# Layer 1's expert rows: added to the output in memory block by block, where they were kept apart and combined at the end

## What is computed

```python
probs = jax.nn.softmax(scores)
weights, idx = jax.lax.top_k(probs, TOP_K)             # TOP_K = 2
weights = weights / jnp.sum(weights, axis=-1, keepdims=True)
out_all = jnp.einsum('tef,edf->ted', silu(xf @ w1) * (xf @ w3), w2)
expert_outs = jnp.take_along_axis(out_all, idx[:, :, None], axis=1)
result = jnp.einsum('tkd,tk->td', expert_outs, weights)
x = x + L1_attn(xn) + result
```

## Time and profile before

| | us |
|---|---|
| three executions: lowest, median, highest | 1772.83, 1775.10, 1778.98 |
| span of the profiled execution, first to last instruction | 1724.1 |
| PE busy in it | 1679.7 (97%) |
| DVE, ACT, POOL busy | 1350.6, 812.6, 609.5 |
| first and last put issued (start) | 1476.6 and 1679.9 |

### The profile page before, as it was taken

The page is one execution under the profiler, slowest core; times in us unless marked ns, Lnnn a source line. Parts: engine busy times, 40 slices in busy tenths (PEclk is TensorE's granted clock), DMA queues, the critical chain, the costliest instruction groups (busy, mean ns, idle before and its releaser), DMA issues.

```text
span 1724.1 us, 24432 instructions
## 1 busy us (share of the span) xinstructions
PE 1679.7 (97%) x7020; PEld 1188.6 (69%) x7020; DVE 1350.6 (78%) x3866; ACT 812.6 (47%) x1456; POOL 609.5 (35%) x656
## 2 busy tenths in 40 slices
PE   5999999999999999999999999999999999999995
PEld 4667777777777777777777777777777766667773
DVE  5878888888888787979797979787888776565558
ACT  4535453636363545454544445454545343554431
POOL 3311242424242324233333232332323233567770
PEclk8999999999999999999999999999999999999998
DMA  8949474646373747373737373645546445577758
GB/s 211 201 104 256 100 187 105 178 109 181 99 181 101 182 103 194 97 200 86 202 84 192 85 189 90 174 106 135 144 106 167 99 109 154 191 266 266 237 173 312
DMA packets 172339, 273.89 MB, mean 159 GB/s; under 512 B 14312, under 2 KB 57320, under 8 KB 171952
## 3 DMA queue, kind: packets, MB, share of 16 engines
q1 hardware_dynamic: 163632, 254.63, 56.1%
q0 software_dynamic: 8576, 17.70, 3.2%
HBM read 202.15 MB, written 65.93 MB: 155 GB/s over the span
## 4 chain that ended last, share of the span: by engine, by line
PE 94%; DVE 2%; ACT 1%; issue 1%; DMA 1%; POOL 0%; SPq 0%; POOLq 0%; DVEq 0%; ACTq 0%
PE ps_y L709 26%; PE ps_gate L660 8%; PE ps_gate L661 8%; PE ps_gate L662 8%; PE ps_up L662 8%; PE ps_up L660 8%; PE ps_up L661 8%; PE ps_y L735 4%; PE ps_side L675 3%; PE ps_side L758 1%; PE ps_side L852 1%; PE ps_side L835 1%; PE ps_side L794 1%; PE ps_side L819 1%; PE ps_side L660 1%; PE ps_side L661 1%
## 5 line engine op out<-in xcount | busy, mean ns | idle before, releaser
L918 DVE TENSOR_TENSOR silu_h<-ps_up,silu_h 128x512 f32<-128x512 f32 x618 | 424.0, 686 | 295.3 <-ACT silu_h L1325 243.3
L1325 ACT ACTIVATE silu_h<-ps_gate 128x512 f32<-128x512 f32 x618 | 367.6, 598 | 567.4 <-PE ps_gate L662 565.1
L709 PE MATMUL ps_y<-silu_h,w_dn 128*128 128x512 f32 x1056 | 542.7, 595 | 3.0 <-DVE silu_h L912 3.0
L912 DVE TENSOR_TENSOR silu_h<-coef_b,silu_h 128x512 f32<-128x512 f32 x528 | 386.8, 732 | 13.0 <-DMA coef_b<-coef_kept 9.2
L660 PE MATMUL ps_gate<-xnT,w_gu 128*128 128x512 f32 x528 | 342.7, 649 | 0.0
L709 PEld LDWEIGHTS ps_y<-silu_h,w_dn 128*128 128x128 f32 x1056 | 199.7, 189 | 53.7 <-issue 7.7
L660 PE MATMUL ps_up<-xnT,w_gu 128*128 128x512 f32 x528 | 207.9, 394 | 4.6 <-DVE silu_h L918 4.6
L661 PE MATMUL ps_gate<-xnT,w_gu 128*128 128x512 f32 x528 | 209.4, 397 | 0.0
L662 PE MATMUL ps_gate<-xnT,w_gu 128*128 128x512 f32 x528 | 208.9, 396 | 0.0
L662 PE MATMUL ps_up<-xnT,w_gu 128*128 128x512 f32 x528 | 208.0, 394 | 0.0
L661 PE MATMUL ps_up<-xnT,w_gu 128*128 128x512 f32 x528 | 206.8, 392 | 0.0
(11 more groups left out here) (267 smaller groups left out, 2454.8 us busy)
## 6 DMA issues: line engine op xcount, KB each, us to landing
coef_b<-coef_kept SPq DMA_DIRECT2D x254, 512.0 KB, 6.8
slots_x<-empty SPq DMA_DIRECT2D x15, 2080.0 KB, 12.7
w_block<-w_kept SPq DMA_DIRECT2D x45, 512.0 KB, 3.9
xs<-slots_x SPq DMA_DIRECT2D x37, 260.0 KB, 3.8
y_back<-y_kept SPq DMA_DIRECT2D x15, 512.0 KB, 7.0
w_down<-in_ffn_w SPq DMA_DIRECT2D x45, 128.0 KB, 3.7
w_raw<-in_ffn_w SPq DMA_DIRECT2D x33, 128.0 KB, 7.9
xres<-in_x SPq DMA_DIRECT2D x16, 256.0 KB, 3.1
```

The lines of the kernel that those rows point to most:

```text
L709: eng.matmul(ps_y[:, :], w_dn[:, j], silu_h[:, g % HBUFS], start=j == 0, stop=last).then_inc(pe_down)
L912: eng.tensor_tensor(silu_h[:, s], coef_b[:, q % COEF_RING, k], silu_h[:, s], ALU.mult).then_inc(dve_h)
L918: eng.tensor_tensor(silu_h[:, s], ps_up[g % 2][:, :], silu_h[:, s], ALU.mult).then_inc(dve_h1)
L1325: eng.activation(silu_h[:, s], ps_gate[g % 2][:, :], ACT.Silu).then_inc(act_silu)
```

## The change

The buffers y_kept and x1_kept are gone, and so are `load_x1`, `load_y`, `combine` and `store_out`. `keep_x1` stores x1 of a chunk straight into the rows of the output (same size and place in SP's list). The number that `send` stores with a row is the token's row, the same for both picks; that of an empty slot is a row of the last chunk, whose rows are stored after everything else. The put is an indirect DMA that adds to the output in memory. As two blocks may add to the same row, the first put of block c waits until the four puts of block c - 1 have landed; the first one of all waits for the 15 stores of x1. DVE computes no row numbers any more: POOL's CAST takes them from xs, and so `load_rows` must also wait for the CAST of the block that was in that place. At the end SP waits for all puts and for `last`, and stores the last chunk.

```diff
 def keep_x1(c):
     eng.wait_ge(*read("mixl", c))
-    eng.dma_start(x1_kept[c].rearrange("(r p) d -> p r d", p=P), xres[:, c % RING]).then_inc(x1_out, 16)
+    eng.dma_start(out_rows[c], xres[:, c % RING]).then_inc(x1_out, 16)
...
-            for c in range(YRING):
-                load_y(c)
-            for c in range(SPARSE):
-                store_out(c)
-                if c + YRING < SPARSE:
-                    load_y(c + YRING)
-                if c == SPARSE - 4:
-                    eng.wait_ge(dve_last, 1)
-                    eng.dma_start(last_rows, xres[:, (CHUNKS - 1) % RING]).then_inc(stored, 16)
-            eng.wait_ge(stored, 16 * CHUNKS)
+            eng.wait_ge(dve_last, 1)
+            eng.dma_start(out_rows[CHUNKS - 1], xres[:, (CHUNKS - 1) % RING]).then_inc(stored, 16)
+            eng.wait_ge(stored, 16)
...
 def load_rows(eng, t):
     if t >= XPLACES:
         eng.wait_ge(*read("ysT", t - XPLACES))
+        eng.wait_ge(pool_y_to, (t - XPLACES) // 2 + 1)
...
 elif what.startswith("put"):
     if r == 0 and c % 2 == 0:
-        eng.wait_ge(dve_y_row, c + n)
+        for t in range(c, c + n):
+            eng.wait_ge(xs_in[t % XPLACES], 16 * (t // XPLACES + 1))
-        eng.tensor_copy(y_to[:, these], y_row[:, these]).then_inc(pool_y_to)
+        eng.tensor_copy(y_to[:, these], xs[:, these, :, P + 1]).then_inc(pool_y_to)
         eng.wait_ge(pool_y_to, c // 2 + 1)
+    if r == 0 and c == 0:
+        eng.wait_ge(x1_out, 16 * SPARSE)
+    elif r == 0:
+        eng.wait_ge(landed[(c - 1) % XPLACES], 16 * ROWS * ((c - 1) // XPLACES + 1))
     if r == 0:
         eng.wait_ge(*read("ysT", c))
-    eng.indirect_dma_start(y_kept, bass.IndirectOffsetOnAxis(y_to[:, c % XPLACES, r:r + 1], 0), ys[:, c % BUFS1, r], None).then_inc(landed[c % XPLACES], 16)
+    eng.indirect_dma_start(out, bass.IndirectOffsetOnAxis(y_to[:, c % XPLACES, r:r + 1], 0), ys[:, c % BUFS1, r], None,
+                           compute_op=ALU.add).then_inc(landed[c % XPLACES], 16)
```

More of the change, by code:

```diff
@@ L58 @@
 ROW1 = P + 2
-COMBINE = UNITS1 - 3
-COMBINED = STEPS - TILES - COMBINE
 KEY0 = 1 << 17
@@ L307, in build_program @@
         ffn0.close()
[L308 to L313, removed]
+        xs = sb("xs", [XPLACES, ROWS, ROW1])
+        xsT = sb("xsT", [XBUFS, 2, CHUNK], FP32R)
         w_block = sb("w_block", [BUFS1, HALVES1, 2, 2, P], FP32R)
@@ L334, in build_program @@
         part_in, w_kept_out = sem("part_in"), sem("w_kept_out")
-        zero_out, x1_out, gates_out, gates_in, x1_in, stored = (sem(n) for n in ("zero_out", "x1_out", "gates_out", "gates_in", "x1_in", "stored"))
+        zero_out, x1_out, gates_out, gates_in, stored = (sem(n) for n in ("zero_out", "x1_out", "gates_out", "gates_in", "stored"))
         sent = [sem("sent0"), sem("sent1")]
@@ L367, in build_program @@
         dve_add, act_msg, pool_heard = (sem(n) for n in ("dve_add", "act_msg", "pool_heard"))
-        act_xshi, dve_y_row, pool_y_to, dve_out, dve_last = (sem(n) for n in ("act_xshi", "dve_y_row", "pool_y_to", "dve_out", "dve_last"))
+        act_xshi, pool_y_to, dve_last = (sem(n) for n in ("act_xshi", "pool_y_to", "dve_last"))
         dve_own = sem("dve_own")
@@ L1259, in step @@
                     eng.tensor_scalar(block_row[:, :], begins[:, :], float(CHUNK), None, ALU.mult).then_inc(dve_table)
-                elif what == "combine":
-                    combine(c)
                 elif what == "last":
@@ L1271, in step @@
                         read("xsT", key)[0])
-                    eng.wait_ge(xs_in[key % XPLACES], 16 * (key // XPLACES + 1))
-                    if key > 0:
-                        eng.wait_ge(dve_y_row, key)
-                    if key >= XPLACES:
-                        eng.wait_ge(pool_y_to, (key - XPLACES) // 2 + 1)
-                    to = xs[:, key % XPLACES, :, P + 1]
-                    keep(eng.tensor_scalar(y_past[:, :], to, float(TOP1 * TOKENS), float(key * CHUNK), ALU.is_ge, ALU.mult))
-                    wait_own()
-                    eng.tensor_tensor(y_row[:, key % XPLACES], to, y_past[:, :], ALU.add).then_inc(dve_y_row)
                 elif what == "ys":
@@ L1287, in step @@
                                       xs[:, key % XPLACES, :, P].unsqueeze(2).to_broadcast([P, ROWS, P]), ALU.mult).then_inc(read("ysT", key)[0])
-            def combine(c):
-                if c == 0:
-                    eng.wait_ge(x1_in, 16 * SPARSE)
-                eng.wait_ge(y_in[c % YRING], 16 * (c // YRING + 1))
-                keep(eng.tensor_tensor(x1_at(c), y_back[:, c % YRING, 0], x1_at(c), ALU.add))
-                wait_own()
-                eng.tensor_tensor(x1_at(c), y_back[:, c % YRING, 1], x1_at(c), ALU.add).then_inc(dve_out)
             eng.memset(minus_half[:, :], -0.5)
@@ L1313, in vector @@
                     step(what, key)
-            for c in range(COMBINED, SPARSE):
-                combine(c)
         def scalar(eng):
@@ L1578, in step @@
                         eng.tensor_copy(rows1[:, c % 2, :, P], gw[:, :, k])
-                        eng.tensor_scalar(rows1[:, c % 2, :, P + 1], row_of, float(k * TOKENS + c * CHUNK), None, ALU.add).then_inc(pool_mark)
+                        eng.tensor_scalar(rows1[:, c % 2, :, P + 1], row_of, float(c * CHUNK), None, ALU.add).then_inc(pool_mark)
                         eng.wait_ge(dve_slot, c + 1)
@@ L1598, in gpsimd @@
                     eng.wait_ge(pool_clear, 1)
-                    eng.tensor_scalar(empty[:, :, P + 1], row_of, float(TOP1 * TOKENS), None, ALU.add).then_inc(pool_clear)
+                    eng.tensor_scalar(empty[:, :, P + 1], row_of, float(SPARSE * CHUNK), None, ALU.add).then_inc(pool_clear)
             for g in range(STEPS):
```

38 lines of the change are left out of this document (4 added, 34 removed).

## The result

The changed kernel takes 1880.0 us (1876.32 to 1881.07, four runs), beside 1775.4 for the kernel before in the same session: ratio 1.0587 [1.0569, 1.0604], slower. The predicted time was 1879.0. That closeness is not what it seems. In a later session the same two kernels gave 1879.8 and 1726.1, ratio 1.0887 [1.0869, 1.0905]: 154 us, where the prediction worked out 104. Of 57 executions of the kernel before in the three later sessions 55 took 1724.8 to 1727.6 us, but one took 1935.5 at a granted clock of 0.84 and one 3504.2; for the four of the first session, 1772.8 to 1779.0, no span or clock is on record that would say what made them longer.

The account below looks back on a forecast made before the run. PE bounds the blocks, DVE and transfers the end; afterwards the chain of landings sets the pace. Span 1511.4 + 36 L = 1828.2 us with L = 8.8, plus 51.0 outside the span: 1879.2 us, range 1805 to 1985.

Parts of the forecast that it names:

- L: Expert blocks: time from one block's first put to the next one's, three issues, a landing and a start; 8.8 us.
- the first put: Start of the expert blocks' first put, claimed to stay at 1476.6 us.
- The distance between span and median: Whole kernel: the median of the runs lies 51.0 us above the profiled span, added to the predicted span.
- rival 2: Adding puts in the blocks much dearer, by more descriptors or serial read-add-write: L above 10.3, time above 1933 us; 26%.
- the lower bound of 6.6: Lowest L for the blocks: issues 3.8, landing 2.5 as for layer 0's plain scatters, start 0.3 us.
- The estimate of L = 6.4: Blocks, priced by the skill's pages: 3.8 + 2.3 + 0.3 us, some 86 us less over 36 steps than with 8.8.
- The removal of the end: End of kernel without kept-row loads and combinations: finishes near 1708, 16 us below the span.
- From X to the end: From the start of the last block's last put (X) to the span's end: 25 + 3 cold start + 3 store, 31 us.
- PE's lead and idle time: Blocks: PE leads by some four blocks, then from about block 8 idles some 3.4 us a block.
- Rival 3, the clock: Blocks: PE's lower clock sets the pace, up to 9.8 us a block, time 1915; counted within the forecast's range.
- Rival 1: Blocks: the adding put lands like a plain one, L between 6.6 and 7.4, time 1800 to 1829 us; 20%.
- Rival 4: Whole kernel faster: the removed end's 16 us outweighs the chain, needing L under 5.9; 3%.

Follow-up runs that it names:

- add-and-wait kernel: Kernel before, with puts that add into their own cleared rows of y_kept and each block's first put waiting for the previous block's landing; 1893.7 us, ratio 1.0961.

## Why the prediction came out as it did

The direction, the chain of landings as the cause and the path by which it reaches PE were right. The time of 1879.0 was right only by luck, because steps failed in opposite directions by nearly the same amount. The span was put at 1828.2 and is 1879.2, 51.0 too little: 41.8 by L, 8.9 by the first put, 1.8 by the last block's three issues, less 1.5 by the time behind the last put. To it 51.0 us outside the span were added, where 1.9 are.

- **The distance between span and median** failed: the 51.0 us "outside the span" were taken as a cost that every execution has. The profiled execution of the same kernel lies 1.6 above its span (1725.64 against 1724.0), and that of the changed kernel 1.9. Without them the forecast would have been 1830. They are not what lies before the first and after the last instruction, as the section on the time before has it. The two figures came from different executions, and in every execution that has both on record the distance is 1.6 to 1.9 us. A gap of 51 should have been treated as unexplained.
- **L** was mis-sized: 8.8 predicted, 9.96 measured, 36 x 1.16 = 42 us too little. Within it the three issues were put at 3 x 1.26 = 3.8 and are 3 x 1.86 = 5.6. The prediction carried costlier issues only as an upper bound, at 0.96 more each, and left them out of the forecast; they are 0.6 more. The landing was put at 3.3 + 1.4 + 0.3 = 5.0 from the last issue and is 3.6 to 4.0 there, 4.4 over all (9.96 - 5.6). So the estimate of 1.4 for reading was too high (0 to 0.4) and that for the issue too low. The test that the text gave itself, "if the four issues are further apart than 1.26, the added price is descriptors", is what came true: rival 2's mechanism at less than rival 2's price. The software queue's packets go the same way, before and after:

```profile
q0 software_dynamic: 8576, 17.70, 3.2%
```

```profile
q0 software_dynamic: 25152, 17.70, 6.8%
```

  The bytes are equal; the 16576 packets more are 112 for each of the 148 puts. That writing them is what takes POOL longer is argued from this, not shown by a run of its own. Two small slips of the sum changed nothing: the lower bound of 6.6 adds a start that its 2.5 already holds, and the ends of the range, L = 6.7 and 11.7, give 1804 and 1984 by the text's formula, not 1805 and 1985.
- **The pages.** In the trace of the kernel before a plain put lands in 2.2 us at the shortest, near the 2.15 of the Trainium skill (DMA: Bandwidth & Descriptors, the anatomy of a DMA on the GpSimd path); the median of 2.7 to 3.3 is above it. For adding puts the measurement is 3.1 at the shortest. The Trainium skill's statement in Collectives: The Full Stack (stop 4, SDMA and CCE) that the addition is free in the DMA engine, at the price of a second read, fits the 0 to 0.4 us found here; it does not speak of the engine that issues, and POOL pays 0.6 for each issue. The estimate of L = 6.4 drawn from both is refuted by 9.96.
- **The first put** was to stay at 1476.6 and came at 1485.5. The edit was costed by its instructions alone, and the moved tiles were not looked at. With the weights' tiles at their old addresses it is 1477.0.
- **The removal of the end**, 16 us: right. Behind the last put the add-and-wait kernel, with combinations, needs 1894.1 - 1849.0 = 45.1, and the changed kernel with tiles in their old places 1867.7 - 1838.7 = 29.0: 16.1.
- **From X to the end**, 31 us: measured 1879.2 - 1849.7 = 29.5. That POOL's list holds the dense units back was foretold, and the kernel with the last puts behind the additions shows it.
- **PE's lead and idle time**: 3.4 us a block was expected from about block 8. In 1600 to 1640 PE is idle for 14.58 of 40 us, 3.4 for each of the 4.2 blocks. It begins earlier: from 1540 to 1560, about block 6, PE works only 12.80 of 20 us.
- **Rival 3, the clock**: the granted clock falls, 0.87 in that stretch and 0.79 from 1640 to 1850, so part of the work is done at the lower level of 1.2 GHz, but PE still waits. Its 25.42 us of work there are 6.0 for each of the 4.2 blocks, well under the 9.4 that a block takes. It does not set the pace.
- **Rival 1** is refuted by the plain puts in the same kernel: L = 7.79 there, 9.95 with the addition. Its mechanism, an adding put that lands like a plain one, was nearly right; what it left out is the longer issue. **Rival 4** needed L under 5.9. Not even plain puts with the wait come near (7.73).

With the measured values the sum gives the span, 1485.5 + 36 x 9.96 + 5.6 + 29.5 = 1879.2. It must, since L was worked out from the same first and last put, so this is no test of its form. The form is borne out by the experiments: the chain, the end and the first put each moved by themselves when their cause was changed.

## What to carry to other kernels

An accumulating transfer moves a combination out of the vector engine, but where two blocks may add to the same row it brings a total order, and each link of it costs the last transfer's landing as well as all its issues; compare that sum with the pace of the stage before the end's 16 us are counted as a gain. Look at what the issuing engine pays for the new kind of transfer, because work on a side engine at 5 of 5.35 us has no room for 0.6 us more in each of four. And when a profiled span and the timed median differ by 3%, find out why before adding the difference to a sum.

## What the runs showed of the hardware

- An indirect DMA of 128 rows of 512 bytes that adds occupies POOL for 1.55 us, against 0.96 when it writes, and has 112 packets more. It lands 3.1/4.0 us (shortest/median) after its issue started, against 2.2/3.0 (both kinds with the wait, in the kernel before). Of this difference of 0.9 to 1.0 the longer issue is 0.6.
- The small CAST on POOL behind an adding put takes 0.76 us, and 0.21 behind a plain one. It reads xs in the changed kernel both with adding and with plain puts, so its source is not the cause. What is, no run shows.
- The addresses of tiles changed the pace of a stage whose instructions are the same: 89.87, 90.07 or 90.46 us a chunk with PE busy for over 99% of the time, up to 9 us over layer 0. Two versions that differ by less than that should be compared with their tiles in the same places.
